# Five graph hops on one core: hop 0 on x itself with the first weight applied to its sums, two chunks interleaved from hop 1 on, no staging buffer, unrolled loops

## What is computed

```python
# x (2048, 128), adj (2048, 2048), all float32; weights 128x128
h = relu(adj @ (x @ W1) + b1)          # hop 0
h = relu(adj @ (h @ W2) + b2)          # hop 1
x = layernorm(x + h)
f1 = adj @ x @ V1                      # hop 2
f2 = adj @ adj @ x @ V2                # hop 3
f3 = adj @ adj @ adj @ x @ V3          # hop 4
x = layernorm(x + (f1 + f2 + f3) / 3)
```

## Time and profile before

| | |
|---|---|
| median of three runs | 260.78 us (260.33 to 261.87) |
| span of the profiled execution, first to last instruction | 259.7 us |
| own time of the profiled execution outside this span | not shown; the median is 1.1 us above the span |
| TensorE busy | 245.6 us, 95% of the span |
| DVE busy | 203.3 us, 78% |
| ACT busy | 175.1 us, 67% |
| GpSimd busy | 11.9 us |
| DMA | 20.40 MB, most of it before 52 us |

### The profile page before, as it was taken

One profiled execution on the slowest core, in us unless ns is written; L12 is line 12 of the kernel. 1 busy time (PEld: TensorE's weight loads), 2 busy tenths in 40 slices (PEclk: granted clock), 3 DMA queues, 4 the chain that ended last, 5 costly groups with the idle time before them and its releaser, 6 DMA issues.

```text
span 259.7 us, 4709 instructions
## 1 busy us (share of the span) xinstructions
PE 245.6 (95%) x1168; PEld 203.5 (78%) x1168; DVE 203.3 (78%) x398; ACT 175.1 (67%) x298; POOL 11.9 (5%) x16
## 2 busy tenths in 40 slices
PE   1999999999999999989999999999999999999990
PEld 1967888888888888868888888888888888888870
DVE  0678979797889999986868687677768696989855
ACT  1687979787667586756767766767667766766620
POOL 1000000000010202020000000000000000202012
PEclk9999999999999999999999999999999999999997
DMA  5999999914000000000000000000000000101011
GB/s 160 302 369 387 387 385 387 386 39 162 0 3 0 0 1 0 1 0 3 1 0 0 0 0 0 0 4 0 0 0 0 0 0 3 42 0 40 0 40 42
DMA packets 11102, 20.40 MB, mean 79 GB/s; under 512 B 1233, under 2 KB 1873, under 8 KB 10961
## 3 DMA queue, kind: packets, MB, share of 16 engines
q1 hardware_dynamic: 11088, 20.26, 21.8%
HBM read 19.20 MB, written 1.05 MB: 78 GB/s over the span
## 4 chain that ended last, share of the span: by engine, by line
PE 90%; DMA 4%; DVE 3%; ACT 1%; issue 1%; SPq 0%; POOLq 0%; POOL 0%; DVEq 0%
PE sums L290 27%; PE sums L264 27%; PE sums L291 27%; PE weighted L239 5%; PE turned L236 2%; DMA adj<-a_t 2%; DMA nodes<-x_t 2%; DVE ring_low L485 1%; PE sums L248 1%; ACT ring_high L379 0%; DVE nodes L432 0%; POOLq L76 0%; POOL rstd L218 0%; PE weighted L317 0%; DVE operand_low L441 0%
## 5 line engine op out<-in xcount | busy, mean ns | idle before, releaser
L485 DVE TENSOR_TENSOR ring_low<-adj,ring_high 128x512 fp32r<-128x512 f32 x240 | 157.2, 688 | 39.8 <-PE sums L264 23.0
L379 ACT ACTIVATE ring_high<-adj 128x512 fp32r (+1 forms) x240 | 145.5, 628 | 42.5 <-PE sums L291 29.5
L290 PE MATMUL sums<-ring_high,operand_high 128*128 128x512 f32 x240 | 95.7, 399 | 1.5 <-DVE operand_low L441 1.2
L264 PE MATMUL sums<-ring_low,operand_high 128*128 128x512 f32 x240 | 93.6, 390 | 0.0
L291 PE MATMUL sums<-ring_high,operand_low 128*128 128x512 f32 x240 | 93.4, 389 | 0.0
L290 PEld LDWEIGHTS sums<-ring_high,operand_high 128*128 128x128 f32 x240 | 45.1, 188 | 11.8 <-DVE operand_low L441 1.6
L264 PEld LDWEIGHTS sums<-ring_low,operand_high 128*128 128x128 f32 x240 | 45.0, 188 | 9.6
L291 PEld LDWEIGHTS sums<-ring_high,operand_low 128*128 128x128 f32 x240 | 45.1, 188 | 8.5
L290 PE MATMUL sums<-resident_high,operand_high 128*128 (+1 forms) x80 | 31.3, 391 | 0.0
L264 PE MATMUL sums<-resident_low,operand_high 128*128 (+1 forms) x80 | 31.2, 390 | 0.0
L291 PE MATMUL sums<-resident_high,operand_low 128*128 (+1 forms) x80 | 31.1, 389 | 0.0
(11 more groups left out here) (37 smaller groups left out, 84.9 us busy)
## 6 DMA issues: line engine op xcount, KB each, us to landing
adj<-a_t SPq DMA_DIRECT2D x48, 256.0 KB, 7.8
nodes<-a_t SPq DMA_DIRECT2D x16, 256.0 KB, 7.4
nodes<-x_t SPq DMA_DIRECT2D x4, 256.0 KB, 4.9
nodes<-x_rows SPq DMA_DIRECT2D x1, 1024.0 KB, 4.8
out_rows<-nodes SPq DMA_DIRECT2D x3, 256.0 KB, 2.5
out_rows<-nodes SPq DMA_DIRECT2D x2, 128.0 KB, 1.9
par<-params SPq DMA_DIRECT2D x1, 192.0 KB, 7.5
par<-params SPq DMA_DIRECT2D x1, 65.0 KB, 6.2
```

Of the source, the lines that this page charges most:

```text
L264: used = nc.tensor.matmul(sums[:, c, :], operand_high[:, hop % 2, k, :], a_low, start=False, stop=(k == TILES - 1))
L290: nc.tensor.matmul(sums[:, c, :], y_high, a_high, start=(k == 0), stop=False)
L379: nc.scalar.activation(ring_high[:, n % RING, :], adj[:, c, n, :], ACT.Copy).then_inc(high_ready, 1)
L485: nc.vector.tensor_tensor(ring_low[:, n % RING, :], adj[:, c, n, :], ring_high[:, n % RING, :].bitcast(F32), ALU.subtract).then_inc(low_re ...
```

## The change

Hop 0 takes x as its operand. x is loaded once, by rows, in four parts between the adjacency tiles, and split from `nodes` (`x_tiles`). The chunk sums, which are then (adj @ x) transposed, are evacuated, multiplied by W1 in one matmul of 128x512 fp32 into a new PSUM bank (`lift`, three steps into the next chunk), get bias and relu on ACT (`relu`), and are multiplied by W2 as before (`post`, seven steps in). `first_product` is gone. A resident tile is loaded straight to the place of its low part, so there is no `staged`, and SyncE waits only for tiles of the chunk before. From hop 1 on TensorE does k = 0 to 11 of chunks 0 and 1, then k = 12 to 15 of both, then chunks 2 and 3. All loops are unrolled, and the waits have semaphores of their own.

```diff
+def hop_order(hop):
+    if hop == 0:
+        return [(c, k) for c in range(CHUNKS) for k in range(TILES)]
+    early = TILES - TPC
+    order = [(c, k) for c in (0, 1) for k in range(early)]
+    order += [(c, k) for c in (0, 1) for k in range(early, TILES)]
+    return order + [(c, k) for c in (2, 3) for k in range(TILES)]
+POST_AFTER = (4, 8, 4, 4)
+LIFT_AFTER, SECOND_AFTER = 3, 7
+def post_step(hop, c):
+    return end_of(hop, c) + (SECOND_AFTER if hop == 0 else POST_AFTER[c])
...
             for k in range(TILES):
+                if k % TPC == 0:
+                    g = k // TPC
+                    part = slice(g * TPC, (g + 1) * TPC)
+                    sp.dma_start(nodes[:, part, :], x_rows[:, part, :]).then_inc(x_in[g], 16)
+                load(0, k)
+            sp.dma_start(par[:, W1:V1], params[:, W1:V1]).then_inc(layer_0_in, 16)
...
+            def lift(c):
+                pe.wait_ge(chunk_evacuated, c + 1)
+                if c == 0:
+                    pe.wait_ge(layer_0_in, 16)
+                else:
+                    pe.wait_ge(chunk_relued, c)
+                nc.tensor.matmul(lifted[:], par[:, W1:W1 + D], chunk_t[:], start=True, stop=True
+                                 ).then_inc(chunk_lifted, 1)
...
+            def relu(c):
+                act.wait_ge(layer_0_in, 16)
+                act.wait_ge(chunk_lifted, c + 1)
+                nc.scalar.activation(chunk_t[:], lifted[:], ACT.Relu, bias=par[:, B1:B1 + 1]).then_inc(chunk_relued, 1)
...
             def evacuate(hop, c):
                 act.wait_ge(chunk_summed, hop * CHUNKS + c + 1)
+                if hop or c:
+                    act.wait_ge(post_multiplied, hop * CHUNKS + c)
...
+            def visits(n):      # ACT, before ring block n
+                for hop, c in chunk_ends(n):
+                    evacuate(hop, c)
+                for c in lifts(n):
+                    relu(c)
+                for hop, c in posts(n, 0):
+                    if hop in (0, 2, 3):
+                        operand_tiles(hop, c)
+                for hop, c in posts(n, 6):
+                    if hop == 1:
+                        operand_tiles(hop, c)
```

More of the change, by code:

```diff
@@ L37 @@
 BLOCKS = GROUPS * STREAMED
+STEPS = CHUNKS * TILES
+STREAMS = CHUNKS * BLOCKS
 RING = 4
@@ L42 @@
 TURNED = (1, 2, 3)
[L43 to L58, removed]
 NORM_STEPS = 4
@@ L168, in load_staged @@
[L168 to L180, removed]
@@ L209, in _ @@
             pool.wait_ge(exponent_ready, 1)
-            with pool.Fori(0, whole_groups) as n:
+            for n in range(whole_groups):
                 pool.wait_ge(norm_step, measured(n))
@@ L240, in post, with low_product @@
                 last.then_inc(post_multiplied, 1)
[L242 to L252, removed]
+            def low_product(hop, n, c, k):
                 j, i = k // (STREAMED + 1), k % (STREAMED + 1)
                 if i < STREAMED:
-                    n = j * STREAMED + i
                     a_low = ring_low[:, n % RING, :]
-                    pe.wait_ge(low_ready, (hop * CHUNKS + c) * BLOCKS + n + 1)
+                    pe.wait_ge(low_ready, n + 1)
                 else:
@@ L268, in low_product, with visits @@
                 return used
-            def chunk(hop, c, before):
-                g = hop * CHUNKS + c
-                for k in range(TILES):
+            def visits(step):
+                for c in range(CHUNKS):
+                    if lift_step(c) == step:
+                        lift(c)
+                for hop in range(HOPS):
+                    for c in range(CHUNKS):
+                        if post_step(hop, c) == step:
+                            post(hop, c)
+            n = 0
+            for hop in range(HOPS):
+                behind = None
+                for at, (c, k) in enumerate(ORDER[hop]):
+                    visits(hop * STEPS + at)
+                    if c == 0 and k % TPC == 0:
+                        pe.wait_ge(operand_low_ready, hop * CHUNKS + k // TPC + 1)
                     j, i = k // (STREAMED + 1), k % (STREAMED + 1)
[L275 to L279, removed]
                     y_high, y_low = operand_high[:, hop % 2, k, :], operand_low[:, hop % 2, k, :]
                     if i < STREAMED:
-                        n = j * STREAMED + i
                         a_high = ring_high[:, n % RING, :]
-                        pe.wait_ge(high_ready, g * BLOCKS + n + 1)
+                        pe.wait_ge(high_ready, n + 1)
                     else:
@@ L293, in chunk @@
                         used.then_inc(high_used, 1)
[L295 to L311, removed]
+                    if behind is not None:
+                        low_product(hop, *behind)
+                    behind = (n, c, k)
+                    if k == TILES - 1:
+                        low_product(hop, *behind).then_inc(chunk_summed, 1)
+                        behind = None
+                    n += i < STREAMED
+            pe.wait_ge(products_added, added(HOPS - 1, CHUNKS - 1) - 1)
             for half in range(HALVES):
@@ new lines, in _ @@
+            n = 0
+            for hop in range(HOPS):
+                for c, k in ORDER[hop]:
+                    j, i = k // (STREAMED + 1), k % (STREAMED + 1)
+                    if hop == 0 and c == 0 and k % TPC == 0:
+                        x_tiles(k // TPC)
+                    if i < STREAMED:
+                        visits(n)
+                        if hop == 0:
+                            act.wait_ge(adj_in[c][j * STREAMED + i], 16)
+                        if n >= RING:
+                            act.wait_ge(high_used, n - RING + 1)
+                            act.wait_ge(low_ready, n - RING + 1)
+                        nc.scalar.activation(ring_high[:, n % RING, :], adj[:, c, j * STREAMED + i, :], ACT.Copy
+                                             ).then_inc(high_ready, 1)
+                        n += 1
+                    elif hop == 0:
+                        act.wait_ge(resident_in[c][j], 16)
+                        nc.scalar.activation(resident_high[:, c, j, :], resident_raw[:, c, j, :], ACT.Copy
@@ L384, in chunk @@
                                              ).then_inc(resident_high_ready, 1)
-            for hop in range(HOPS):
-                chunk(hop, 0, (hop - 1, CHUNKS - 1) if hop else None)
-                with act.Fori(1, CHUNKS) as c:
-                    chunk(hop, c, (hop, c - 1))
             act.wait_ge(chunk_summed, HOPS * CHUNKS)
+            act.wait_ge(post_multiplied, HOPS * CHUNKS - 1)
             for half in range(HALVES):
@@ L436, in operand_tiles @@
             def operand_tiles(hop, c):
+                part = slice(c * TPC, (c + 1) * TPC)
                 dve.wait_ge(operand_high_ready, (hop + 1) * CHUNKS + c + 1)
-                high, low = (o[:, (hop + 1) % 2, bass.ts(c, TPC), :] for o in (operand_high, operand_low))
-                source = {0: weighted[:], 1: nodes[:, bass.ts(c, TPC), :]}.get(hop, turned[:])
-                split = nc.vector.tensor_tensor(low, source, high.bitcast(F32), ALU.subtract)
-                if hop < 2:
-                    split.then_inc(taken_over, 1)
@@ L445, in post_step @@
-            def post_step(n, hop, c):
-                for step in DVE_STEPS[hop].get(n, ()):
-                    if step == "residual":
-                        residual(c)
-                    elif step == "operand":
-                        operand_tiles(hop, c)
-                    elif step == "products":
-                        add_products(hop, c)
-                    elif step == "stats":
-                        if hop == 1:
-                            dve.wait_ge(residual_added, c + 1)
-                        else:
-                            dve.wait_ge(taken_over, (hop + 1) * CHUNKS + c + 1)
-                        norm_stats(range(c * TPC, (c + 1) * TPC))
-                    else:
-                        n = c if hop == 1 else CHUNKS + c
-                        {"moments": norm_moments, "apply": norm_apply}[step](n, range(c * TPC, (c + 1) * TPC))
@@ L465, in first_tiles @@
[L465 to L487 removed]
+                high, low = operand_high[:, (hop + 1) % 2, part, :], operand_low[:, (hop + 1) % 2, part, :]
@@ new lines, in operand_tiles, with x_tiles @@
+                source = {0: weighted[:], 1: nodes[:, part, :]}.get(hop, turned[:])
+                nc.vector.tensor_tensor(low, source, high.bitcast(F32), ALU.subtract).then_inc(operand_low_ready, 1)
+            def x_tiles(g):
+                part = slice(g * TPC, (g + 1) * TPC)
+                dve.wait_ge(operand_high_ready, g + 1)
+                nc.vector.tensor_tensor(operand_low[:, 0, part, :], nodes[:, part, :],
+                                        operand_high[:, 0, part, :].bitcast(F32), ALU.subtract
+                                        ).then_inc(operand_low_ready, 1)
@@ new lines, in _ @@
+            n = 0
+            for hop in range(HOPS):
+                for c, k in ORDER[hop]:
```

(21 more changed lines are left out.)

211 lines of the change are left out of this document (116 added, 95 removed).

## The result

The changed kernel takes 263.64 us, the median of four runs (263.15 to 263.91), against 260.88 before. The ratio is 1.011 with a 95% interval of 1.009 to 1.013: 1.1% slower. Forecast were 261.3 us and a range of 258.9 to 263.8. The time lies inside the range, near its upper end, but outside the forecast's own 260.2 to 262.4; the forecast's own 0.2% was a fifth of what came.

A forecast was written before the change was run, and what follows sets the result against it. TensorE, busy for 95% of the span, was taken as the bound. Terms -3.6 + 0.1 + 3.2 - 1.5 + 2.1 + 0.2 = +0.5 took span 259.7 to 260.2; plus 1.1, 261.3 us, range 258.9 to 263.8.

The forecast's parts named there:

- The start: Chunk 0 of hop 0: last tile lands at 18.5, TensorE ends at 20.2, gain 3.6 us (bounds 1.5 to 4.0).
- rival 2: Chunk 0's last tile lands only at 20.5, transfers being slower; gain 1.5 instead of 3.6, 263.4 us; chance 0.15.
- The lift: Four added fp32 matmuls of 128x512 in hop 0 at 0.93 each, less 3 x 0.16 at posts: +3.2 us.
- So it doesn't wait: At each lift, TensorE arrives 1.81 us after a chunk's end, ACT has evacuated by 0.95: no wait.
- The turn: From hop 1 to hop 2, chunk 3's operand is needed at step 24, not 12: TensorE's 1.46 goes, -1.5 us.
- the interleave: In hop 1, closer posts make DVE late near blocks 35, 38 and 47 by 0.2, 1.0 and 0.9: +2.1 us.
- Rivals 1 and 3: DVE in hop 1: 1, it keeps up, 259.0 us, chance 0.20; 3, falls further behind, 263.0 to 263.8, 0.13.
- In hop 4: Same DVE walk, without low operand and with posts 0.43 longer, leaves 0.2 us of waiting (0 to 0.8).
- Unrolling: nothing to gain: All loops written out: looped and straight chunks both take 12.24 us, so no gain was expected.
- rival 4: Unrolling pays: 0.18 us per taken branch in 15 looped chunks gives 2.7, 258.6 us; chance 0.05.
- The base: Whole kernel: span 259.7 before, with the median taken to stand 1.1 us above the span.

The follow-up runs named there:

- e6: The changed kernel with nine fp32 matmuls of 128x128 on the identity, of no use to the result, ahead of hop 0 on TensorE: 263.15 us.
- e5: The kernel before with every hardware loop written out and nothing else changed: 260.45 us.
- e1: The changed kernel with the chunks of every hop in plain order and post steps at the blocks of the kernel before: 262.61 us.
- e4: The changed kernel with ACT's evacuation of hop 0's first chunk before ring block 14 in place of 16: 262.65 us.
- e10: The changed kernel with both the interleave in hop 2 alone (e2) and the earlier first evacuation (e4): 260.29 us.
- e9: The changed kernel with x @ W1 ahead of everything in place of lifts, resident tiles still loaded straight to their place, interleave in hop 2 alone: 258.11 us.
- e12: The kernel of e9 with ten useless fp32 matmuls of 128x128 on the identity ahead of the first product: 257.86 us.
- e7: The changed kernel with x @ W1 products at steps 0, 2, 6 and 10 of hop 0 in place of lifts, new loads and interleave kept: 264.21 us.
- e3: The changed kernel without the four lift matmuls, W1 left out of the computation: 259.74 us.
- e2: The changed kernel with two chunks interleaved in hop 2 alone, hops 1, 3 and 4 plain with posts four steps in: 261.09 us.
- e11: The kernel of e9 with eight useless fp32 matmuls of 128x128 on the identity ahead of the first product: 257.94 us.

## Why the prediction was right, and where it was off

**The start: near.** Forecast 20.2 for the end of chunk 0, measured 20.61, a gain of 3.2 where the sum had 3.6. That arrivals bind it, not TensorE's pace, fits e6. The term was sized by the last tile, whose landing was right (18.55 for 18.5, so rival 2's 20.5 falls). What bound was the fourth part of x, the sixteenth of the twenty transfers: at the forecast's own rate it lands at 15.5, and it landed at 15.94.

Even the 3.2 is more than a usual execution gains. The profiled execution of before was a slow one, and slow in its start: e5, whose chunk 0 is the same straight code, has its first mark at 22.64, not 23.36. The six traces that share the changed start (the changed kernel, e1 to e4, e10) have it at 19.9 to 20.3. The usual gain is then 2.3 to 2.8 us, if e5's trace is a usual one.

What made the gain is mostly that no product stands ahead of chunk 0 any more. e9 keeps x @ W1 first and drops only the staging: its mark, 22.34, is 0.3 below e5's and 1.0 below before's. Taking x as the operand moves it by 2.2 more, to 20.16, and the lifts are the price. These are single executions; e12, where the products run at full pace, has its mark at 20.96, so a good part of the 2.2 is TensorE's slow pace in the products. My theory for e7, that the staging alone had made the gain, was wrong in this.

**The lift: right** in size, 0.93 against 0.90 (e3) and 0.86 in the chain. Net for hop 0 it is a loss: 3.2 gained ahead, 3.1 given back by lifts, 1.1 lost at the first of them.

**"So it doesn't wait": the step that failed.** I took the moment at which ACT evacuates from a row of hop 1, where it idles before the evacuation. At the end of chunk 0 ACT is behind its tiles, and the evacuation stands in its queue behind ring block 15, whose tile lands at 22.04. It starts 2.1 us after TensorE has gone on to chunk 1. Cost 1.07 us where I had 0.1 for this boundary; e4 takes 0.74 of it back in the traces, 1.0 in the medians. The 0.33 that stay are a wait for a ring block that now stands behind the evacuation.

**The turn and the interleave: right.** The turn's gap of 1.46 went, and DVE's lateness in hop 1 came to 0.25, 0.87 and 0.73, 1.85 in all, and 2.1 with about 0.1 at each restart of TensorE (98.53 to 98.86 where 0.23 is the pace), for 0.2, 1.0 and 0.9 forecast. Rivals 1 and 3 fall with this. e1 and e2 tell this from every cause in the rest of the code. In hop 4 0.28 for 0.2.

**"Unrolling: nothing to gain": half right.** The 12.24 are equal, but hop 0 gains 0.15 per chunk (e5). The sum had this amount under another name, so it didn't change. With it rival 4 falls at its size of 2.7 us. The Trainium skill ("Runtime: NRT & Kernel Launch", Instruction fetch mechanics) has a stall at a taken branch whose target isn't in the window that is already fetched; no such stall shows in hops 2 to 4, looped and written out 12.24 both, and whether the targets lay in the window no run here shows.

**The base: 0.5 us off.** I read the span 259.7 as 1.1 below the executions' time. Later runs give spans and times together: 1.8 apart for the kernel before, 1.6 for the changed one, and the median span before is 259.0 to 259.1. The profiled execution of before was 0.6 to 0.7 above this. The right way was to compare like with like: 259.7 + 1.8 = 261.5 for it, and with the changed kernel's 1.6 the forecast span of 260.2 gives 261.8 us.

**The sum in spans:** -3.2 at the start, +1.1 at the first lift, +3.1 for lifts, -1.5 at the turn, +2.1 in hop 1, +0.3 in hop 4, +0.2 behind the last mark and 0.1 in remainders: 2.2, from 259.7 to 261.9; forecast 0.5. Of the 2.3 us between 261.3 and 263.64, 1.7 lie there, 1.0 of them at the one boundary and 0.4 at the start, and 0.5 in the base. So the sum was right in kind, and what it lacked was the one wait; that the time stayed in the range is owed to the width that rivals 2 and 3 had given it.

The gain that the change aims at is there. It was spent on four more matmuls, on an evacuation that waits behind a tile it doesn't need, and on ring blocks that wait behind a normalization. e9 keeps what helps (direct loads of resident tiles, the interleave at the turn to hop 2, unrolled loops) and drops the lifts: 258.11 us, 1.0% faster than the kernel before and 2.1% faster than the changed one.

## What to carry to other kernels

Price a moved operation on every queue it passes, at the place where it will stand: an evacuation that idles in one hop stands behind a late tile in another, and a product set by TensorE's place can stop an engine that runs four blocks ahead of it. A reordering that cures one stall should be tried only where that stall is; bunched posts overfill the engine that had 3% to spare. And don't take a span and a median of different executions for one base.

## What the runs showed of the hardware

TensorE's pace at the start depends on what it did before, while the profile gives the granted clock as full all along. With eighteen records on the identity from 1.52 to 5.3 us ahead, it was at full pace at 6.59 (e6). With sixteen, ending at 5.3 and followed by work at 5.85, it was not, and the slow pace stayed until about 11 us, when the products were nearly done (e11). With twenty up to 6.15, it came to full pace at about 6.9 us, within the first eight records of the products (e12). Each of these is one execution. The slow pace is 0.43 us for a matmul that takes 0.23 later, near the ratio of the two levels of 1.2 and 2.4 GHz.

One fp32 matmul of 128x512 (two records) costs TensorE 0.86 us in the chain and 0.90 in e3, as much as four of 128x128 (eight records, 0.89).
